# First gather pass of a two-layer graph network: the summed source rows move from PSUM to SBUF

## What is computed

```
edge_index = stack([src, dst])
h = relu(layernorm(x));  x = x + L0(h, edge_index, weight)
h = relu(layernorm(x));  x = x + L1(h, edge_index, edge_attr, ...)

L0: h = mobius_matvec(weight, h)
    dist = sqdist(h[edge[0]], h[edge[1]])
    ... edge_e = f(dist);  h_e = logmap0(h)
    h_prime = segment_sum(edge_e[:, None] * h_e[edge[1]], edge[0])
    out = proj(expmap0(elu(h_prime / segment_sum(edge_e, edge[0]))))
```

## Time and profile before

| | |
|---|---|
| median of three runs | 18782.42 us |
| range of the three | 18748.07 to 19046.77 us |
| the profiled execution's own time | 18755.79 us |
| its span | 18754.0 us |
| granted TensorE clock, mean | 0.602 |

### The profile page before, as it was taken

The page is one execution under the profiler, slowest core; times in us unless marked ns, Lnnn a source line. Parts: engine busy times, 40 slices in busy tenths (PEclk is TensorE's granted clock), DMA queues, the critical chain, the costliest instruction groups (busy, mean ns, idle before and its releaser), DMA issues. The chain is left out here.

```text
span 18754.0 us, 142433 instructions
## 1 busy us (share of the span) xinstructions
PE 4880.6 (26%) x28224; PEld 3611.6 (19%) x28225; DVE 7656.7 (41%) x14407; ACT 2119.6 (11%) x4439; POOL 11223.1 (60%) x12446
## 2 busy tenths in 40 slices
PE   0000000000011111111111882232323232328997
PEld 0000000000000000000000881111111111113996
DVE  5779600000133333333335884333333333336775
ACT  2000000000000000000000760000000000005333
POOL 0267777777666666666662772666666666650773
PEclk6555555555555555555555995566556556569998
DMA  2000000000122222222223441222222222257331
GB/s 51 3 4 5 5 5 5 5 5 5 35 73 73 71 73 72 72 73 73 73 73 37 140 136 35 65 69 64 67 65 67 66 66 67 66 71 234 106 106 59
DMA packets 770958, 1143.40 MB, mean 61 GB/s; under 512 B 322012, under 2 KB 469339, under 8 KB 770652
## 3 DMA queue, kind: packets, MB, share of 16 engines
q1 hardware_dynamic: 386972, 666.22, 11.7%
q0 software_dynamic: 322304, 245.26, 8.4%
q10 hardware_dynamic: 61632, 231.44, 3.1%
HBM read 872.56 MB, written 269.54 MB: 61 GB/s over the span
## 5 line engine op out<-in xcount | busy, mean ns | idle before, releaser
L1323 POOL DMA_INDIRECT big<-b_d,big x3424 | 3278.0, 957 | 2274.6 <-POOLq L140 1239.6
L854 POOL DMA_INDIRECT big<-h_d,big x3424 | 3270.4, 955 | 1832.2 <-issue 1100.1
L607 POOL DMA_INDIRECT rec_d<-big x3224 | 3099.3, 961 | 1608.1 <-issue 983.6
L889 PE MATMUL ps<-big 128*128 x3424 | 740.3, 373 | 8746.8 <-PEq L140 5220.7
L889 PEld LDWEIGHTS ps<-big 128*128 128x128 bf16 x3424 | 442.5, 162 | 9044.4 <-issue 9041.7
L908 DVE TENSOR_REDUCE ps<-ps 128x260 f32<-128x780 f32 x856 | 837.6, 978 | 3278.8 <-remote 1441.9
L1450 DVE TENSOR_REDUCE ps<-ps 128x256 f32<-128x768 f32 x856 | 827.6, 967 | 2541.0 <-DVEq L140 1383.9
L1649 POOL TENSOR_SCALAR big<-iota_f,big 128x128 f32<-128x128 f32 x1498 | 875.3, 604 | 842.5 <-DMA big<-rec_d 528.5
L1402 PE MATMUL ps<-big 128*128 x3424 | 610.0, 336 | 2752.9 <-issue 2286.3
L628 DVE CAST big<-big 128x896 f32 (+2 forms) x9 | 8.3, 918 | 2778.4 <-DMA big<-h_d 2777.4
L1402 PEld LDWEIGHTS ps<-big 128*128 128x128 bf16 x3424 | 444.7, 159 | 3112.4 <-issue 3112.3
(11 more groups left out here) (347 smaller groups left out, 9734.5 us busy)
## 6 DMA issues: line engine op xcount, KB each, us to landing
big<-e_d SPq DMA_DIRECT2D x428, 512.0 KB, 3.2
rows_d<-big ACTq DMA_DIRECT2D x214, 544.0 KB
big<-rows_d SPq DMA_DIRECT2D x214, 544.0 KB, 3.3
HA<-slots_d SPq DMA_DIRECT2D x214, 512.0 KB
big<-slots_d SPq DMA_DIRECT2D x214, 512.0 KB
e_d<-big ACTq DMA_DIRECT2D x214, 512.0 KB
big<-rec_d SPq DMA_DIRECT2D x860, 64.0 KB, 3.0
big<-h_d,big POOLq DMA_INDIRECT x3424
```

What stands on the lines that cost most here:

```text
L607: gp.indirect_dma_start(rec_d, bass.IndirectOffsetOnAxis(ix_stage[b][:, j:j + 1], 0), rec_stage[b][:, j * REC:(j + 1) * REC], None).then_i ...
L854: gp.indirect_dma_start(G[g][:, t * ROW:(t + 1) * ROW], None, h0_d, bass.IndirectOffsetOnAxis(idx[g % 2][:, t:t + 1], 0)).then_inc(gath[g] ...
L889: m = t.matmul(XS[q % 2][:, n, 0:3 * D + 3], OT3[g % 2][:, o, :], T0[:, ds(chunks[o // 2] * TW, 3 * D + 3)], start=True, stop=True)
L1323: gp.indirect_dma_start(G[g][:, t * D:(t + 1) * D], None, b_d, bass.IndirectOffsetOnAxis(idx[g % 2][:, t:t + 1], 0)).then_inc(gath[g], 16)
```

## The change

`xrow` is taken from SBUF in place of PSUM. It is one line:

```diff
         XS = [ps[:, h * 1024:(h + 1) * 1024].rearrange("p (t w) -> p t w", w=256) for h in range(2)]
-        xrow = ps[:, 2048:2048 + TB * (D + 1)].rearrange("p (t w) -> p t w", w=D + 1)
+        xrow = take(TB * (D + 1)).rearrange("p (t w) -> p t w", w=D + 1)
```

## The result

| | before | after |
|---|---|---|
| median | 18765.4 us (12 runs) | 18736.72 us (12 runs) |
| lowest to highest | 18748.07 to 19046.77 | 18723.06 to 18747.41 |
| profiled execution | 18755.79 us | 18726.59 us |
| its span | 18754.0 us | 18724.8 us |

The ratio is 0.9984, with a 95% interval of 0.9977 to 0.9992: 29 us less. The highest time before, 19046.77 us, belongs to a slower state that some executions of either kernel show, and is left out of the ratio. The result is within 2% and inside the range, but the likeliest case was 18,840 us, slower than before. The sign was wrong.

What follows compares the result with a forecast made beforehand. The prediction took POOL's gathers, about four blocks and then one 13.4 us rest, to bound the first gather pass. Held gathers added 70 us, other terms 0: 18,826 us profiled, 18,852 on the median, given as 18,840; range 18,730 to 19,050.

Steps and rivals of the forecast that it cites:

- POOL sets when they do: First gather pass: PE and DVE hold POOL back, but POOL's gathers set when; 93 us per four blocks against 95.6 measured.
- They show that groups come quickly once POOL has rested some 8 us, and that POOL rests only because its four buffers are full: First gather pass: about four blocks of gathers (80 us), then a 13.4 us rest, 8.4 us of it until PE is released.
- every microsecond that is added to POOL while it runs is added to the pass: First gather pass: time added to running POOL lengthens the pass in full, so all 70 us of held gathers count.
- the +70 us of the sum: Gathers held at their start by L914 with two SBUF inputs: 145 starts x 0.48 us; bounds 0 and 160 us.
- The hold itself: In the first gather pass, L914 with two SBUF inputs delays gathers starting within it: 145 starts, 0.48 us each on the mean.
- the branch by which the sum would have been nil: If a gather doesn't count as a GpSimd operation that reads SBUF, L914 holds no gather and the 70 us are nil.
- The formula: Held time of a gather or scatter start: rest of the DVE operation then, less about 0.13 us; those under way aren't held.
- the bounds: Per call: L908 0 to 12 ns less; L914 no change, 10 ns of rounding; L916 30 ns less to 20 more.
- The 966 ns for L908: Reduces writing SBUF: 966 ns in place of 978, 10 us at most over 856 calls; taken as 0.
- The 65 ns a call: Copies and L914 shorter by the skill's 58 against 120 fixed cycles: 14 us over 214 calls of one; not counted.
- Rival A: Holds are hidden: gathers aren't held, or POOL's 13.4 us rests take them up; 18,756 to 18,782 us, chance 0.28.
- Rival C: Faster than 2%: holds act as pauses that let PE's groups through, so POOL's rests vanish; 18,120 us, chance 0.04.
- Rival B: Slower than 2%: held starts split the cycle into two rests per four blocks; 19,360 us, milder 19,100; chance 0.10.

Runs made afterwards that it cites:

- e3: Kernel before with two memsets of 1150 words, each waited for, on POOL after each block's 16 gathers: 18716.81 us against 18645.14 on the second chip.
- c4: Kernel before with one memset of 8 words and a wait on POOL after each block's 16 gathers: 18703.11 us against 18731.07 on the fifth chip.

## Why the prediction was wrong

- **What bounds the pass.** "POOL sets when they do" was half right. POOL's stream of gathers does bring the slow groups with it, since breaks of 3.43 us between blocks end them (e3), but the same stream runs without slow groups on two chips. "They show that groups come quickly once POOL has rested some 8 us, and that POOL rests only because its four buffers are full" described the rows; the conclusion drawn from it failed.
- **The step that failed** is "every microsecond that is added to POOL while it runs is added to the pass", and with it the +70 us of the sum. On the first chip 46 us more of busy time came with 76 us less of idle time. The prediction had read itself that L914 waits for no gather (55.3 us over 214 calls); the pass ends when DVE has had its groups from PE, and those did not come later for POOL's holds. On the chips with slow groups 208 us of breaks cost nothing (c4), and 754 us of breaks in place of POOL's waits cost 72 us (e3). Where POOL has no waits the step holds: 256 us of gaps came with 252 us. For the holds of 13 to 15 us it is likely but not shown (medians 9 to 15 us up, the pass in the traces 2 and 6 us).
- **The hold itself** was right in its mechanism, rule and size: rest less 0.12 to 0.13 us, 142 held starts against 145 forecast, 59.7 us against 70. By the rule of the Trainium skill (SBUF — State Buffer, the section on its two separate sides) a gather thereby counts as an operation that reads SBUF, as the scatters did; the branch by which the sum would have been nil is out. The result without a loss comes from POOL's rests and not from the absence of holds. The formula was incomplete for L898, which also draws out gathers already under way.
- **L908, L914, L916**: -7, +2 and -3 ns, all within the bounds. The 966 ns for L908 were worked out with 1.04 ns an element, where the rows beside it gave 0.99 and so 978 again; 971 lies between. The 65 ns a call that the Trainium skill's fixed costs would give (VectorE: DVE Perf Modes, trn2 errata) aren't there: 1227 ns from SBUF, 1225 from PSUM.
- **Rival A** came nearest on the first chip: held, and hidden, with 18,756 to 18,782 us for it; measured 18,737. Its condition, that the slow groups don't hang on POOL, is not so (e3), and what it lacks is the gain of 29 to 37 us, which came all three times on chips with slow groups. That 18,737 lies inside the range at all is luck: its lower end of 18,730 was an allowance for low runs, and no case of the prediction led there.
- **Rival C** (pauses let PE's groups through) was dismissed because L898's holds do nothing of the kind. A break of 3.43 us at every block does just that, so the mechanism exists; but that holds of 0.4 us are a small dose of it is a guess. For it: the gain is clear of noise only in kernels with holds in L914, and shows as less idle time of POOL. Against it: the multiply alone has nearly the same holds and gave 1.0003 and 0.9988; and the slow groups are not fewer, 374 waits of the reduces over 1.5 us before and 370 after on the first chip, 370 and 374 on the fifth.
- **Rival B** has no sign: 67 waits, not more than 69.

What stays open: why the change as a whole gains 0.2% where the groups are slow, whether any part alone does (the multiply alone did on one chip of two), and what makes the groups slow on some chips. Register loads were tried and are not it.

## What to carry to other kernels

Before a stall is added to an engine's path, ask whether that engine ever waits: where POOL had 730 us of waits, holds of 60 us vanished in them; where it had none, added gaps of 256 us cost 252. A DVE multiply with both inputs in SBUF held nearly every gather that started with over 0.2 us of it to go (142 of 161 starts here), and none with one input in PSUM; so the place in PSUM is worth keeping only where POOL has no slack. And a gain of 0.2% on one chip was none on another, perhaps a loss of up to 0.1%: time such a change on more than one.

## What was not expected of the hardware

The same kernel takes 18,645 to 18,768 us on four chips and 17,008 to 17,024 us on two, with the same instruction times. The difference lies in waits: 3279 us of DVE before the reduces against 260 us in this pass. It is in the scatter stage too; there L513 waits in the trace of the kernel before ("remote" is a release whose source the profile doesn't hold),

```profile
L513 DVE COPY_PREDICATED big<-big,ps x396: 431/912/1949, 616.0 to 2173.4; 128x248 f32<-128x248 uint16 x50, 128x868 f32<-128x868 uint16 x50, 128x496 f32<-128x496 uint16 x49, 128x1612 f32<-128x1612 uint16 x49
...
  remote: 130.7, 41
```

and not at all on the third chip (the changed kernel, with the same L513), where its last one starts at 2001 us:

```profile
L513 DVE COPY_PREDICATED big<-big,ps x396: 430/912/1948, 620.0 to 2001.4; 128x248 f32<-128x248 uint16 x50, 128x868 f32<-128x868 uint16 x50, 128x496 f32<-128x496 uint16 x49, 128x1612 f32<-128x1612 uint16 x49
```

The granted clock does not explain it: 0.602 against 0.616 over the span, and 0.50 in this pass on the first and on the fourth chip. On the chips with slow groups SP's own short instructions are stretched as well, most by 0.7 us: 625 of them last over 0.3 us between 5200 and 9000 us of the trace before, none on the third and fourth chip, and none with the 3.43 us break on the second. The long waits of the reduces come in the same steps: those over 8.7 us bunch near 8.8, 9.5, 10.2 and 10.9 us. So it is not PE alone that is held up on these chips while POOL issues gathers without a break.
